# Context rows of the later three batches centred, turned and multiplied with W in two passes of 128 and 103 rows in place of three of 77

## The chip, the cores and the metric

The kernel runs on one core of a Trainium2 chip. The metric is the device time of one execution in microseconds (us). TensorE (PE in the profile) multiplies, and its weight loads are listed apart as PEld. VectorE is DVE, ScalarE is ACT, GpSimd is POOL, and SyncE (SP) only issues DMAs here.

## What is computed

For 4 batches of 2048 tokens with 512 features, each token attends over the 77 context rows of its batch, and a linear layer follows. Both branches are normalised first and both are added back with a gate:

```python
def _L0_xattn_ref(hidden_states, visual_hidden_state):
    fusion_scores = jnp.einsum('bsd,bvd->bsv', hidden_states, visual_hidden_state)
    fusion_probs = jax.nn.softmax(fusion_scores, axis=-1)
    fusion_output = jnp.einsum('bsv,bvd->bsd', fusion_probs, visual_hidden_state)
    return fusion_output
...
x = x + jnp.tanh(g_xattn[0]) * _L0_xattn_ref(_layernorm(x, axis=-1), ctx_1024)
x = x + jnp.tanh(g_ffn[0]) * _L0_ffn_ref(_layernorm(x, axis=-1), L0_ffn_W, L0_ffn_b, L0_ffn_lora_down, L0_ffn_lora_up, L0_ffn_down_aux, L0_ffn_up_aux)
return x
```

`_L0_ffn_ref` multiplies with W plus a low-rank product and adds a bias. All numbers are float32.

## The kernel before

The tokens are cut into T = 64 tiles of 128 rows, TB = 16 tiles to a batch. One loop, `all_tiles`, runs on every engine over t = 0 to 63; `step(t, k)` is the work of a tile, with parts of tiles t - 1, t - 2 and t + 2 laid beside it by hand. The order on each engine is exactly the order of the code, and engines meet through semaphores.

In a step TensorE multiplies the tile's two float parts (a high part and a rest, in `xT`) with `wc`, which holds W side by side with the centred and turned context rows of the batch (24 matmuls, L555). It turns the softmax weights of the tile before (`p_transpose`, L563) and multiplies them with `stacks` (6 matmuls, L581 and L586). `stacks` holds the gated context rows v and their product with W, v*W, each as a high part and a rest, spread by copies over the partitions so that two matmuls take all products; it has two halves, for even and odd batches.

What each batch needs of its context is prepared in the second half of the batch before, by the `prep` functions and a few lines of `step`, at fixed tiles t % 16: rows read and scaled at 8 (STATS) and 9 (ROWS), centred at 10 (CENTRE, DVE L677), turned by four TensorE transposes at 11 (TURN, L522) and taken from PSUM into `ct` by ACT (L394) and DVE (L682), multiplied with W at 12 (PRODUCT, twelve matmuls of 512 columns, L531), and the product taken into `v_hi` and `v_lo` at 13 (TAKE). At 15 (SWITCH) ACT copies `ct` into the columns of `wc` (`ctx_columns`, two copies, L401). This happens three times, each time with 77 rows (V). Batch 0 is prepared before the loop.

The DMAs that matter all go through the one queue of SyncE. It works by units of two tiles. `unit(u)` waits for the output of tiles 2u and 2u + 1, stores it, and loads x (`load_x`) and turned x (`load_xt`) of unit u + 4 into the place that has come free:

```python
for u in range(B * NU - 1):
    n, k = u // NU, u % NU
    if n < B - 1:
        if k == 1:

            sp.wait_ge(v_lo_ok, 2 * n + 2)
            load_ctx(n + 1)
        if k == NU - 2:
            stack(n + 1)
    unit(u)
```

So the next batch's context rows (`c_rows`, 77 rows of 2 KB) are loaded ahead of units 1, 9 and 17, and `v_hi` and `v_lo` are copied into `stacks` by five DMAs (77, 13, 64, 13 and 64 rows of 4 KB, `stack`) ahead of units 6, 14 and 22. ACT converts the turned x of tile t + 2 in step t (`x_hi`, L408) and waits there for that unit's load; it does so ahead of writing the softmax weights of tile t (`probabilities`, L430), for which TensorE's next `p_transpose` waits.

Of the kernel before, what the change touches and what calls it, by code (L numbers as in the profile page):

```python
# [19 lines left out]
def build_kernel(nc, x, xt_in, ctx_in, W, b_gates, low_in, low_out, out):  # L20
# [18 lines left out]
    FIRST = DMAS + 1  # L39
    assert TB == 2 * HB and V + R <= 96 and D == 512  # L40

# [3 lines left out]
    with ExitStack() as stack:  # L45
# [28 lines left out]

        c_rows = sb("c_rows", [V, D])
        c_bn = sb("c_bn", [V, 6])
        c_mv = sb("c_mv", [V, 2])
        c_cent = sb("c_cent", [V, D])
        ct = sb("ct", [P, 2, KC, V], F32R)
        v_hi = sb("v_hi", [V, 2 * D], F32R)  # L80
        v_lo = sb("v_lo", [V, 2 * D], F32R)

# [25 lines left out]
        c_ps = ps("c_ps", [P, D])  # L108
        ct_ps = c_ps[:, 0:KC * V].rearrange("p (c v) -> p c v", c=KC)

# [21 lines left out]
        def cw_ps(n):  # L132

            return a_ps[0:V, :] if n == 0 else c_ps[0:V, :]

# [32 lines left out]
        def all_tiles(step, prep, until=T + 1):  # L168

            for t in range(until):  # L170
                step(t, t)
                if t % TB >= HB and t < T - TB:
                    prep(t // TB + 1, t % TB)

        def switches(t, k):

            return t % TB == k and t < T - TB

        def real(t):
# [15 lines left out]
        def stack_landed(n):  # L195

            return 16 * (DMAS * (n // 2 + 1) + (FIRST - DMAS if n % 2 == 0 else 0))

# [10 lines left out]
        def _(sp):  # L209
# [11 lines left out]
            def stack_hi(n, cols):  # L221

                hi, to = v_hi[:, cols].bitcast(F32), stacks[:, n % 2, :, cols].bitcast(F32)
                for rows, source in ((to[0:V, 0, :], hi), (to[96:K0, 0, :], hi[Q:V, :]), (to[0:Q, 1, :], hi[0:Q, :])):
                    sp.dma_start(rows, source).then_inc(stacked[n % 2], 16)

            def stack_lo(n, cols):

                lo, to = v_lo[:, cols].bitcast(F32), stacks[:, n % 2, :, cols].bitcast(F32)
                for rows, source in ((to[V:V + R, 0, :], lo[Q:V, :]), (to[Q:P, 1, :], lo[0:Q, :])):  # L230
                    sp.dma_start(rows, source).then_inc(stacked[n % 2], 16)

# [5 lines left out]

            def stack(n):

                if n < 2:
                    sp.wait_ge(zeroed, 1)
                else:
                    sp.wait_ge(y_ready, TB * (n - 1))
                sp.wait_ge(v_hi_ok, 2 * n + 1)
                stack_hi(n, slice(0, 2 * D))
                sp.wait_ge(v_lo_ok, 2 * n + 2)
                stack_lo(n, slice(0, 2 * D))

# [19 lines left out]
            sp.wait_ge(v_hi_ok, 1)  # L269
            stack_hi(0, slice(0, D))  # L270
# [4 lines left out]
            stack_lo(0, slice(0, D))  # L275
            first_stack_lo()
# [23 lines left out]
        def _(pool):  # L300
# [9 lines left out]
            def first_columns():  # L310

                pool.wait_ge(ct_lo_ok, 1)
                for part in range(2):
                    pool.tensor_copy(wc[:, :, part, D:D + V], ct[:, part, :, :].bitcast(F32)).then_inc(c_cols, 1)

# [51 lines left out]
        def _(act):  # L367
            act.dma_start(b_row[:, D:D + 2], b_gates[D:D + 2].partition_broadcast(P)).then_inc(ld_gates, 16)
            act.dma_start(c_rows[:, :], ctx_in[0]).then_inc(ld_ctx, 16)
            act.dma_start(low_out_sb[:, :], low_out).then_inc(ld_out, 16)  # L370
# [5 lines left out]
            def ctx_rows_hi(n):  # L376

                act.wait_ge(ld_ctx, 16 * n + 16)
                if n == 0:
                    act.wait_ge(tg_ok, 1)  # L380
                else:
                    act.wait_ge(stacked[(n - 1) % 2], stack_landed(n - 1))
                act.activation(v_hi[:, 0:D], c_rows[:, :], ACT.Copy, scale=tg[0:V, 0:1]).then_inc(v_hi_ok, 1)

            def ctx_product_hi(n):

                act.wait_ge(cw_mm, n + 1)
                act.activation(v_hi[:, D:2 * D], cw_ps(n), ACT.Copy, scale=tg[0:V, 0:1]).then_inc(v_hi_ok, 1)

            def prep(n, k):  # L390
                if k == TURN:

                    act.wait_ge(c_tr, n + 1)
                    act.activation(ct[:, 0, :, :], ct_ps, ACT.Copy).then_inc(ct_hi_ok, 1)  # L394

            def ctx_columns(n):

                act.wait_ge(s_ready, TB * n)
                act.wait_ge(ct_lo_ok, n + 1)
                for part in range(2):  # L400
                    act.activation(wc[:, :, part, D:D + V], ct[:, part, :, :].bitcast(F32), ACT.Copy).then_inc(c_cols, 1)  # L401

# [37 lines left out]
            def step(t, k):  # L440
# [12 lines left out]
                if real(t - 1) and t != T - 1:  # L453
                    variance(t - 1, k - 1)
                if switches(t, STATS):
                    ctx_rows_hi(t // TB + 1)
                if switches(t, TAKE):
                    ctx_product_hi(t // TB + 1)
# [44 lines left out]
        def _(pe):  # L503
# [11 lines left out]
            def prep(n, k):  # L515
                if k == TURN:

                    pe.wait_ge(c_centred, n + 1)
                    if n:
                        pe.wait_ge(v_lo_ok, 2 * n)  # L520
                    for c in range(KC):
                        mm = pe.transpose(ct_ps[:, c, :], c_cent[:, c * P:(c + 1) * P], ident[0:V, 0:V])  # L522
                    mm.then_inc(c_tr, 1)
                if k == PRODUCT:
# [4 lines left out]
                    for c in range(KC):  # L529
                        for lhs, rhs in ((0, 0), (0, 1), (1, 0)):  # L530
                            mm = pe.matmul(cw_ps(n), ct[:, lhs, c, :], wc[:, c, rhs, 0:D],  # L531
                                           start=(m == 0), stop=(m == 3 * KC - 1))
                            m += 1
                    mm.then_inc(cw_mm, 1)

            def first_product():

                pe.wait_ge(ct_lo_ok, 1)
                for c in range(KC + 1):
                    if c < KC:  # L540
                        pe.wait_ge(w_hi_ok, c + 1)
                        for lhs in range(2):
                            pe.matmul(cw_ps(0), ct[:, lhs, c, :], wc[:, c, 0, 0:D], start=(c == 0 and lhs == 0),  # L543
                                      stop=False)
                    if c:
                        pe.wait_ge(w_lo_ok, c)
                        mm = pe.matmul(cw_ps(0), ct[:, 0, c - 1, :], wc[:, c - 1, 1, 0:D], start=False, stop=(c == KC))  # L547
                mm.then_inc(cw_mm, 1)
# [42 lines left out]
            def step(t, k):  # L591
                if real(t):
# [4 lines left out]
                    if k % TB == 0:  # L597
                        pe.wait_ge(c_cols, 2 * (t // TB) + 2)
                    x_product(t, k, 1, range(0, 1))
# [54 lines left out]
        def _(dve):  # L654
            dve.memset(expd[:, :, :], 0.0).then_inc(expd_ok, 1)

            def ctx_rows_lo(n):

                dve.wait_ge(c_own, 2 * n + 1)
                dve.wait_ge(v_hi_ok, 2 * n if n else 1)  # L660
                dve.scalar_tensor_tensor(out=v_lo[:, 0:D], in0=c_rows[:, :], scalar=tg[0:V, 0:1],
                                         in1=v_hi[:, 0:D].bitcast(F32), op0=ALU.mult, op1=ALU.subtract)\
                    .then_inc(v_lo_ok, 1)

            def ctx_mean(n):
                dve.bn_aggr(c_mv[:, :], c_bn[:, :]).then_inc(c_own, 1)

            def prep(n, k):
                if k == STATS:
                    dve.wait_ge(ld_ctx, 16 * n + 16)  # L670
                    dve.bn_stats(c_bn[:, :], c_rows[:, :]).then_inc(c_own, 1)
                if k == ROWS:
                    ctx_rows_lo(n)
                    ctx_mean(n)
                if k == CENTRE:
                    dve.wait_ge(c_own, 2 * n + 2)
                    dve.tensor_scalar(c_cent[:, :], c_rows[:, :], c_mv[:, 0:1], None, ALU.subtract)\  # L677
                        .then_inc(c_centred, 1)
                if k == TURN:

                    dve.wait_ge(ct_hi_ok, n + 1)
                    dve.tensor_tensor(ct[:, 1, :, :], ct_ps, ct[:, 0, :, :].bitcast(F32), ALU.subtract)\  # L682
                        .then_inc(ct_lo_ok, 1)
                if k == TAKE:

                    dve.wait_ge(v_hi_ok, 2 * n + 1)
                    dve.scalar_tensor_tensor(out=v_lo[:, D:2 * D], in0=cw_ps(n), scalar=tg[0:V, 0:1],
                                             in1=v_hi[:, D:2 * D].bitcast(F32), op0=ALU.mult, op1=ALU.subtract)\
                        .then_inc(v_lo_ok, 1)
# [169 lines left out]
```

## Time and profile before

| | |
|---|---|
| median of three runs | 313.3 us (312.91 to 313.48) |
| the profiled execution, its own time | 313.07 us |
| its span (first to last instruction) | 311.3 us |
| TensorE matmul busy | 302.0 us, 97% of the span |
| VectorE, ScalarE, GpSimd busy | 75%, 60%, 73% |
| DMA traffic | 56.39 MB, 181 GB/s on the mean |

Busy shares are means over the span. The granted TensorE clock is given as a share of 2.4 GHz, and its mean is 0.995. A profile's rows name source lines of the kernel before. The profiled execution took 0.2 us less than the median, and 1.8 us of it lie outside the span.

### The profile page before, as it was taken

The page shows a single profiled execution, that of the slowest core. Times are in us where ns is not written, and L with a number is a line of the kernel's source. Part 1 is how long each engine was busy: PE and PEld are TensorE (multiplying, and loading weights), DVE is VectorE, ACT ScalarE, POOL GpSimd, SP SyncE. Part 2 cuts the span into 40 slices and gives each one's busy share as a digit, 9 for nine tenths or more (in the row PEclk, how much of TensorE's full clock was granted, in tenths as well). Part 3 has the DMA queues.
Part 4 walks back from the last instruction along what each step waited for, and adds up shares of the span by engine and source line. Part 5 has one row for each costly group of instructions (what it writes and reads, how often), then busy time and mean ns, then how long its engine had stood idle before and what let it go on. Part 6 is the DMA issues. An engine that isn't in the chain of part 4 may idle for free.

```text
span 311.3 us, 6483 instructions
## 1 busy us (share of the span) xinstructions
PE 302.0 (97%) x2086; PEld 286.1 (92%) x2086; DVE 235.0 (75%) x743; ACT 187.5 (60%) x546; POOL 226.5 (73%) x276
## 2 busy tenths in 40 slices
PE   5999999999999999999999999999999999999992
PEld 3779999998999999999899999999899999999992
DVE  2887778895787887798497778888588777777765
ACT  3665656664576656666466566656466656566552
POOL 3747887788487777877577877778478778877763
PEclk9999999999999999999999999999999999999998
DMA  5845455345594455555294565544197554444013
GB/s 162 305 147 225 151 187 175 149 174 205 182 272 175 166 187 177 204 202 205 73 266 192 202 226 202 204 171 162 76 274 254 203 201 150 169 179 170 27 59 135
DMA packets 16614, 56.39 MB, mean 181 GB/s; under 512 B 2129, under 2 KB 2129, under 8 KB 16580
## 3 DMA queue, kind: packets, MB, share of 16 engines
q1 hardware_dynamic: 15856, 54.64, 50.5%
q10 hardware_dynamic: 724, 1.32, 1.3%
q8 instruction: 17, 0.28, 0.4%
q14 instruction: 17, 0.14, 0.1%
HBM read 35.84 MB, written 16.78 MB: 169 GB/s over the span
## 4 chain that ended last, share of the span: by engine, by line
PE 94%; DMA 2%; DVE 1%; ACT 1%; issue 0%; POOLq 0%; ACTq 0%; POOL 0%; DVEq 0%
PE y_ps L555 66%; PE y_ps L586 10%; PE a_ps L581 10%; PE c_ps L531 3%; PE y_ps L563 2%; DMA c_rows<-in_ctx 2%; PE y_ps L626 1%; PE y_ps L631 1%; PE a_ps L543 1%; PE c_ps L522 1%; PE y_ps L647 0%; PE a_ps L547 0%; PE y_ps L508 0%; DVE o_sb L753 0%; DVE v_lo L818 0%
## 5 line engine op out<-in xcount | busy, mean ns | idle before, releaser
L555 PE MATMUL y_ps<-wc,xT 128*128 128x334 f32 (+1 forms) x1536 | 228.2, 302 | 0.0
L555 PEld LDWEIGHTS y_ps<-wc,xT 128*128 128x128 f32 x1536 | 214.4, 189 | 2.1
L334 POOL TENSOR_TENSOR x_bias<-x,bias_g 128x512 f32<-128x512 f32 x63 | 81.4, 1292 | 63.1 <-DVE x L715 63.1
L322 POOL TENSOR_TENSOR xT<-xt_raw,xT 128x512 fp32r<-128x512 f32 x64 | 83.1, 1298 | 0.1
L423 ACT ACTIVATE expd<-y_ps,neg_max,rs 128x77 f32<-128x77 f32 x64 | 26.6, 416 | 80.2 <-DVE neg_max L705 80.2
L437 ACT ACTIVATE squares<-x,x_nmean 128x512 f32<-128x512 f32 x64 | 46.4, 725 | 16.4 <-DVE x_nmean L723 16.4
L350 POOL TENSOR_TENSOR rs<-stat_eps,half_neg 128x2 f32<-128x2 f32 (+1 forms) x67 | 46.0, 687 | 5.2
L753 DVE SCALAR_TENSOR_TENSOR o_sb<-y_ps,rs,x_bias 128x512 f32<-128x512 f32 x64 | 48.0, 750 | 1.4 <-issue 0.8
L586 PEld LDWEIGHTS y_ps<-stacks,pT 109*128 109x128 f32 (+1 forms) x256 | 39.8, 191 | 5.4
L715 DVE SCALAR_TENSOR_TENSOR x<-a_ps,x_sb 128x512 f32<-128x512 f32 x64 | 43.6, 682 | 0.2 <-PE a_ps L581 0.2
L694 DVE BATCH_NORM_STATS2 bn<-x_sb 128x6 f32<-128x512 f32 x64 | 43.8, 684 | 0.0
L736 DVE TENSOR_TENSOR pT<-y_ps,pT 13x128 fp32r<-13x128 f32 x62 | 18.0, 291 | 32.1 <-ACT pT L414 32.1
L586 PE MATMUL y_ps<-stacks,pT 109*128 109x256 f32 (+1 forms) x256 | 41.0, 282 | 0.0
L581 PE MATMUL a_ps<-stacks,pT 109*128 109x512 f32 (+1 forms) x128 | 40.3, 396 | 0.0
L408 ACT ACTIVATE xT<-xt_raw 128x512 fp32r<-128x512 f32 x63 | 39.2, 622 | 0.0
L702 DVE TENSOR_REDUCE s_max<-y_ps 128x1 f32<-128x77 f32 x64 | 14.9, 233 | 20.7 <-PE y_ps L555 20.3
L430 ACT ACTIVATE p_ext<-expd,e_inv 128x154 f32<-128x154 f32 x64 | 26.5, 414 | 0.7 <-DVE e_inv L730 0.5
L414 ACT ACTIVATE pT<-y_ps 96x128 fp32r<-96x128 f32 x62 | 16.5, 266 | 9.6 <-PE y_ps L563 8.7
L581 PEld LDWEIGHTS a_ps<-stacks,pT 109*128 109x128 f32 (+1 forms) x128 | 19.7, 190 | 0.2 <-issue 0.2
L739 DVE TENSOR_TENSOR pT<-y_ps,pT 64x128 fp32r<-64x128 f32 x62 | 17.5, 283 | 1.9
L415 ACT ACTIVATE pT<-y_ps 64x128 fp32r<-64x128 f32 x62 | 16.6, 268 | 1.5
L563 PE MATMUL y_ps<-ident,p_ext 128*96 128x128 f32 x62 | 16.8, 271 | 0.5 <-ACT p_ext L430 0.5
(80 smaller groups left out, 193.7 us busy)
## 6 DMA issues: line engine op xcount, KB each, us to landing
x_sb<-in_x SPq DMA_DIRECT2D x32, 512.0 KB, 4.2
xt_raw<-in_xt SPq DMA_DIRECT2D x31, 512.0 KB, 5.1
out<-o_sb SPq DMA_DIRECT2D x31, 512.0 KB, 3.0
stacks<-v_hi SPq DMA_DIRECT2D x3, 308.0 KB
stacks<-v_hi SPq DMA_DIRECT2D x3, 256.0 KB
stacks<-v_lo SPq DMA_DIRECT2D x3, 256.0 KB
w_rows<-in_w SPq DMA_DIRECT2D x2, 256.0 KB, 6.1
w_rows<-in_w ACTq DMA_DIRECT2D x2, 256.0 KB, 6.8
```

What stands on the lines that cost most here:

```text
L322: pool.tensor_tensor(xT[:, k % TRING, 1, :, :], xt_raw[:, k % XRING // UNIT, k % UNIT, :, :], xT[:, k % TRING, 0, :, :].bitcast(F32), ALU. ...
L334: pool.tensor_tensor(x1_bias[:, q, :], x1[:, j, :], bias_g[:, :], ALU.add).then_inc(x1b_ready, 1)
L350: pool.tensor_tensor(rs[:, q, a:b], stat_eps[:, q, a:b], half_neg[:, a:b], ALU.pow).then_inc(rs_ready, 1)
L408: act.activation(xT[:, k % TRING, 0, :, :], xt_raw[:, k % XRING // UNIT, k % UNIT, :, :], ACT.Copy)\
L423: act.activation(expd[:, j, 0:V], scores(k), ACT.Exp, bias=neg_max[:, j:j + 1], scale=rs[:, k % 4, 0:1], accum_out=e_sum[:, j:j + 1]).then ...
L437: act.activation(squares[:, k % 2, :], x1[:, k % 2, :], ACT.Square, bias=x1_nmean[:, k % 2:k % 2 + 1], scale=D ** -0.5, accum_out=stat[:, ...
L555: mm = pe.matmul(y_half(k, h)[:, 0:n], xT[:, k % TRING, part, c, :], wc[:, c, w, h * H:h * H + n], start=(c == 0 and part == 0 and w == 0) ...
L581: mm = pe.matmul(a_ps[:, :], pT[0:rows[s], k % 2, s, :], stacks[0:rows[s], pair, s, 0:D], start=(s == 0), stop=(s == 1))
L586: mm = pe.matmul(y_half(k, h)[:, 0:H], pT[0:rows[s], k % 2, s, :], stacks[0:rows[s], pair, s, D + h * H:D + (h + 1) * H], start=False, sto ...
L694: dve.bn_stats(bn[:, k % 2, :], x_sb[:, k % XRING, :]).then_inc(bn_ok, 1)
L715: dve.scalar_tensor_tensor(out=x1[:, j, :], in0=a_ps[:, :], scalar=1.0, in1=x_sb[:, k % XRING, :], op0=ALU.mult, op1=ALU.add, accum_out=x1 ...
L753: dve.scalar_tensor_tensor(out=o_sb[:, q, :].rearrange("p (h d) -> p h d", h=2), in0=y_both(k), scalar=rs[:, (k + 3) % 4, 1:2], in1=x1_bia ...
```

## The change

The context rows of batches 1, 2 and 3 (231 rows) are handled in two passes: 128 rows (batch 1, and 51 rows of batch 2, here TAIL) in the second half of batch 0, and 103 rows (26 of batch 2, 77 of batch 3) in the second half of batch 1. In the second half of batch 2 nothing is prepared but the columns of `wc`. `ct` is kept twice, `c_rows`, `v_hi`, `v_lo` are 128 rows high, and the copies into `stacks` are cut and moved to match.

```diff
+    PACK = (V, P, (B - 1) * V - P)
+    TAIL = P - V
...
-        ct_ps = c_ps[:, 0:KC * V].rearrange("p (c v) -> p c v", c=KC)
+        ct_all = c_ps[:, :].rearrange("p (c v) -> p c v", c=KC)
...
-                if t % TB >= HB and t < T - TB:
+                if t % TB >= HB and t < T - 2 * TB:
                     prep(t // TB + 1, t % TB)
...
             def load_ctx(n):
-                sp.dma_start(c_rows[:, :], ctx_in[n:n + 1].rearrange("o v d -> (o v) d")).then_inc(ld_ctx, 16)
...
+                at = V + (n - 1) * P
+                sp.dma_start(c_rows[0:PACK[n], :], ctx_in.rearrange("b v d -> (b v) d")[at:at + PACK[n], :])\
+                    .then_inc(ld_ctx, 16)
...
+            def stack_head(n):
+
+                both = slice(0, 2 * D)
+                copy(n, slice(0, TAIL), 0, v_hi, V, both)
+                copy(n, slice(0, TAIL), 1, v_hi, V, both)
+                copy(n, slice(Q, Q + TAIL), 1, v_lo, V, both)
...
+            def stack_rest(n):
+
+                both = slice(0, 2 * D)
+                copy(n, slice(TAIL, V), 0, v_hi, 0, both)
+                copy(n, slice(96, K0), 0, v_hi, Q - TAIL, both)
+                copy(n, slice(TAIL, Q), 1, v_hi, 0, both)
+                copy(n, slice(V, V + R), 0, v_lo, Q - TAIL, both)
+                copy(n, slice(Q + TAIL, P), 1, v_lo, 0, both)
...
-                if n < B - 1:
-                    if k == 1:
-
-                        sp.wait_ge(v_lo_ok, 2 * n + 2)
-                        load_ctx(n + 1)
-                    if k == NU - 2:
-                        stack(n + 1)
+                if n < 2 and k == 1:
+                    sp.wait_ge(v_lo_ok, 2 * n + 2)
+                    load_ctx(n + 1)
+                if n == 0 and k == NU - 2:
+                    rows_cast(1)
+                    stack_hi(1, 0, slice(0, 2 * D))
+                    stack_lo(1, 0, slice(0, 2 * D))
+                if n == 1 and k == 1:
+                    sp.wait_ge(y_ready, TB)
+                    stack_head(2)
+                if n == 1 and k == NU - 2:
+                    rows_cast(2)
+                    stack_rest(2)
+                if n == 2 and k == 1:
+                    sp.wait_ge(y_ready, 2 * TB)
+                    stack_hi(3, V - TAIL, slice(0, 2 * D))
+                    stack_lo(3, V - TAIL, slice(0, 2 * D))
                 unit(u)
...
+                if n == 2:
+                    act.wait_ge(stacked[0], 16 * (FIRST + 3))
...
+                    if n == 2:
+                        act.activation(wc[:, :, part, D:D + TAIL], ct[:, 1, part, :, V:P].bitcast(F32), ACT.Copy)\
+                            .then_inc(c_cols, 1)
+                        act.activation(wc[:, :, part, D + TAIL:D + V], ct[:, 0, part, :, 0:V - TAIL].bitcast(F32), ACT.Copy)\
+                            .then_inc(c_cols, 1)
```

Three places show how the order moves. First the DMA queue of SyncE at the start of batch 1, before the change; the rows are from the store of unit 8 to the loads of unit 14 (output, x, turned x, and the context rows):

```order
L254 DMA out<-o_sb 128x1024 [waits out_ready]
L211 DMA x_sb<-in_x 128x1024
L215 DMA xt_raw<-in_xt 128x1024 [waits xl_ready]
L219 DMA c_rows<-in_ctx 77x512 [waits v_lo_ok]
L254 DMA out<-o_sb 128x1024 [waits out_ready]
L211 DMA x_sb<-in_x 128x1024
L215 DMA xt_raw<-in_xt 128x1024 [waits xl_ready]
```

The same place of the same queue after the change:

```order
L288 DMA out<-o_sb 128x1024 [waits out_ready]
L229 DMA x_sb<-in_x 128x1024
L233 DMA xt_raw<-in_xt 128x1024 [waits xl_ready]
L238 DMA c_rows<-in_ctx 103x512 [waits v_lo_ok]
L243 DMA stacks<-v_hi 51x1024 [waits y_ready]
L243 DMA stacks<-v_hi 51x1024
L243 DMA stacks<-v_lo 51x1024
L288 DMA out<-o_sb 128x1024 [waits out_ready]
L229 DMA x_sb<-in_x 128x1024
L233 DMA xt_raw<-in_xt 128x1024 [waits xl_ready]
```

The context load has 103 rows in place of 77, and three copies of 51 rows now stand between it and the store of unit 9 and the loads of unit 13.

TensorE in the second half of batch 2, before the change; from the second step shown, four transposes of the centred context stand ahead of a tile, and twelve matmuls of the product a step later:

```order
L581 MATMUL a_ps<-stacks,pT 128x512 x2
L586 MATMUL y_ps<-stacks,pT 128x256 x4
L555 MATMUL y_ps<-wc,xT 128x256 x6
L522 MATMUL c_ps<-ident,c_cent 128x77 x4
L555 MATMUL y_ps<-wc,xT 128x334 x3
L563 MATMUL y_ps<-ident,p_ext 96x128
L555 MATMUL y_ps<-wc,xT 128x334 x9
L555 MATMUL y_ps<-wc,xT 128x256 x6
L581 MATMUL a_ps<-stacks,pT 128x512 x2
L586 MATMUL y_ps<-stacks,pT 128x256 x4
L555 MATMUL y_ps<-wc,xT 128x256 x6
L531 MATMUL c_ps<-wc,ct 77x512 x12
```

The same place after the change:

```order
L635 MATMUL a_ps<-stacks,pT 128x512 x2
L640 MATMUL y_ps<-stacks,pT 128x256 x4
L609 MATMUL y_ps<-wc,xT 128x256 x6
L609 MATMUL y_ps<-wc,xT 128x334 x3
L617 MATMUL y_ps<-ident,p_ext 96x128
L609 MATMUL y_ps<-wc,xT 128x334 x9
```

The four transposes and the twelve matmuls are gone from this batch and nothing takes their place. In the two passes that stay, the transposes are 128x128 and 128x103 and the product 128x512 and 103x512, at the same places as before.

## Rows read from the trace of the kernel before

**Rows 1.** Waits of TensorE in the loop: us in total, times, longest

```profile
PE y_ps L563 <- ACT p_ext L430: 0.5, 1, 0.5
```

**Rows 2.** The chain that ended last: start us, us, what (third pass)

```profile
206.72 2.10 PE y_ps L555 x15
...
211.05 2.09 PE y_ps L555 x15
...
215.69 2.09 PE y_ps L555 x15
...
222.81 2.09 PE y_ps L555 x15
```

**Rows 3.** Timeline of TensorE, five places: start us, us, line, tile, shape

```profile
7.72 0.78 PE L522 MATMUL c_ps<-ident,c_cent 77*128 77x77 f32 x4 [0.50 <-DVE c_cent L677]
...
68.33 0.63 PE L581 MATMUL a_ps<-stacks,pT 109*128 109x512 f32 x2
...
69.99 0.43 PE L522 MATMUL c_ps<-ident,c_cent 77*128 77x77 f32 x4
...
146.95 2.96 PE L531 MATMUL c_ps<-wc,ct 128*77 128x512 f32 x12
...
305.08 0.64 PE L586 MATMUL y_ps<-stacks,pT 109*128 109x256 f32 x4
```

**Rows 4.** Groups by shape: xcount, busy us, mean ns of one, idle before

```profile
L581 PE MATMUL a_ps<-stacks,pT 109*128 109x512 f32 x64 | 25.3, 395 | 0.0
...
L581 PEld LDWEIGHTS a_ps<-stacks,pT 128*128 128x128 f32 x64 | 12.2, 190 | 0.0
...
L531 PEld LDWEIGHTS c_ps<-wc,ct 128*77 128x77 f32 x36 | 5.1, 145 | 2.6
...
L812 DVE SCALAR_TENSOR_TENSOR wc<-y_ps,tg,wc 128x512 fp32r<-128x512 f32 x4 | 2.8, 747 | 1.0 <-ACT wc L497 0.9
...
L821 DVE SCALAR_TENSOR_TENSOR stacks<-a_ps,tg,stacks 64x512 fp32r<-64x512 f32 x1 | 0.7, 744 | 0.0
```

**Rows 5.** Timeline of ACT and of weight loads in step 31

```profile
160.56 0.81 ACT L401 ACTIVATE wc<-ct 128x308 fp32r<-128x308 f32 x2 [0.44 <-PE y_ps L555]
...
162.19 0.41 ACT L430 ACTIVATE p_ext<-expd,e_inv 128x154 f32<-128x154 f32 x1
...
163.04 0.13 PEld L563 LDWEIGHTS y_ps<-ident,p_ext 128*96 128x96 f32 x1
```

**Rows 6.** DMA packets from 115.3 to 123.9, 106.7 to 115.3, 80.8 to 97 us

```profile
DMA packets 432, 1.57 MB, mean 183 GB/s; under 512 B 48, under 2 KB 48, under 8 KB 432
...
DMA packets 522, 1.76 MB, mean 204 GB/s; under 512 B 59, under 2 KB 59, under 8 KB 520
...
DMA packets 1165, 4.11 MB, mean 254 GB/s; under 512 B 165, under 2 KB 165, under 8 KB 1164
```

**Rows 7.** Windows: busy by engine; the last three are PEclk, DMA share, GB/s

```profile
84.00:85.00 1.00, 1.00 (x9) 0.92 (x8) 0.96 (x4) 0.05 (x1) 1.00 (x1) 1.00 1.00 401
...
87.00:88.00 1.00, 1.00 (x8) 1.00 (x7) 0.71 (x4) 0.77 (x4) 0.92 (x3) 1.00 1.03 160
...
112.00:113.00 1.00, 1.00 (x9) 0.97 (x8) 0.70 (x2) 0.97 (x3) 1.00 (x1) 1.00 0.46 160
...
308.00:309.00 1.00, 0.00 (x0) 0.00 (x0) 0.75 (x1) 0.00 (x0) 0.00 (x0) 0.69 0.68 258
```

**Rows 8.** Timeline around units 9 and 13: SyncE's queue, ACT, weight loads

```profile
108.46 0.41 SPq L219 DMA_DIRECT2D c_rows<-in_ctx  x1
...
116.30 0.79 SPq L215 DMA_DIRECT2D xt_raw<-in_xt  x1
...
128.09 0.62 ACT L408 ACTIVATE xT<-xt_raw 128x512 fp32r<-128x512 f32 x1
128.61 0.42 ACT L430 ACTIVATE p_ext<-expd,e_inv 128x154 f32<-128x154 f32 x1
...
129.65 0.12 PEld L563 LDWEIGHTS y_ps<-ident,p_ext 128*96 128x96 f32 x1
```

More of the change, by code:

```diff
@@ L39, in build_kernel @@
     FIRST = DMAS + 1
-    assert TB == 2 * HB and V + R <= 96 and D == 512
+    PACK = (V, P, (B - 1) * V - P)
+    TAIL = P - V
+    assert TB == 2 * HB and V + R <= 96 and D == 512 and B == 4 and 0 < TAIL < Q and V <= PACK[2] <= P
     x_units = x.rearrange("b (u p n) d -> (b u) p n d", p=P, n=UNIT)
@@ L73, in build_kernel @@
         wc = sb("wc", [P, KC, 2, D + VP], F32R)
[L75 to L81, printed above, removed]
+        c_rows = sb("c_rows", [P, D])
+        c_bn = sb("c_bn", [P, 6])
+        c_mv = sb("c_mv", [P, 2])
+        c_cent = sb("c_cent", [P, D])
+        ct = sb("ct", [P, 2, 2, KC, P], F32R)
+        v_hi = sb("v_hi", [P, 2 * D], F32R)
+        v_lo = sb("v_lo", [P, 2 * D], F32R)
         stacks = sb("stacks", [P, 2, 2, 2 * D], F32R)
@@ L132, in cw_ps @@
         def cw_ps(n):
-            return a_ps[0:V, :] if n == 0 else c_ps[0:V, :]
+            return a_ps[0:V, :] if n == 0 else c_ps[0:PACK[n], :]
         def up_bank():
@@ L177, in switches, with packs, columns_done @@
             return t % TB == k and t < T - TB
+        def packs(t, k):
+            return t % TB == k and t < T - 2 * TB
+        def columns_done(n):
+            return 2 * n + 2 + (2 if n >= 2 else 0)
         def real(t):
@@ L195, in stack_landed @@
         def stack_landed(n):
-            return 16 * (DMAS * (n // 2 + 1) + (FIRST - DMAS if n % 2 == 0 else 0))
+            return 16 * (FIRST, DMAS, FIRST + 3 + DMAS, 2 * DMAS)[n]
         def unit_turn(t, k, ring):
@@ L218, in load_ctx, with copy, stack_hi, stack_lo @@
             def load_ctx(n):
-                sp.dma_start(c_rows[:, :], ctx_in[n:n + 1].rearrange("o v d -> (o v) d")).then_inc(ld_ctx, 16)
[L221 to L231, printed above, removed]
+                at = V + (n - 1) * P
+                sp.dma_start(c_rows[0:PACK[n], :], ctx_in.rearrange("b v d -> (b v) d")[at:at + PACK[n], :])\
+                    .then_inc(ld_ctx, 16)
+            def copy(n, rows, s, source, at, cols):
+                sp.dma_start(stacks[rows, n % 2, s, cols].bitcast(F32),
+                             source[at:at + rows.stop - rows.start, cols].bitcast(F32)).then_inc(stacked[n % 2], 16)
+            def stack_hi(n, at, cols):
+                copy(n, slice(0, V), 0, v_hi, at, cols)
+                copy(n, slice(96, K0), 0, v_hi, at + Q, cols)
+                copy(n, slice(0, Q), 1, v_hi, at, cols)
+            def stack_lo(n, at, cols):
+                copy(n, slice(V, V + R), 0, v_lo, at + Q, cols)
+                copy(n, slice(Q, P), 1, v_lo, at, cols)
+            def stack_head(n):
[10 more added lines that the diff above has]
+                copy(n, slice(Q + TAIL, P), 1, v_lo, 0, both)
             def first_stack_lo():
@@ L530, in prep @@
                         for lhs, rhs in ((0, 0), (0, 1), (1, 0)):
[L531 removed]
+                            mm = pe.matmul(cw_ps(n), ct_part(n, lhs)[:, c, :], wc[:, c, rhs, 0:D],
                                            start=(m == 0), stop=(m == 3 * KC - 1))
@@ L542, in first_product @@
                         for lhs in range(2):
-                            pe.matmul(cw_ps(0), ct[:, lhs, c, :], wc[:, c, 0, 0:D], start=(c == 0 and lhs == 0),
+                            pe.matmul(cw_ps(0), ct_part(0, lhs)[:, c, :], wc[:, c, 0, 0:D], start=(c == 0 and lhs == 0),
                                       stop=False)
@@ L546, in first_product @@
                         pe.wait_ge(w_lo_ok, c)
-                        mm = pe.matmul(cw_ps(0), ct[:, 0, c - 1, :], wc[:, c - 1, 1, 0:D], start=False, stop=(c == KC))
+                        mm = pe.matmul(cw_ps(0), ct_part(0, 0)[:, c - 1, :], wc[:, c - 1, 1, 0:D], start=False, stop=(c == KC))
                 mm.then_inc(cw_mm, 1)
```

59 lines of the change are left out of this document (31 added, 28 removed).

## Prediction

> **What bounds the kernel now.** I read the waits of TensorE first. In the whole loop it waits once, for 0.5 us in the first step [rows 1]; after that it never stands still until the last tiles. The chain of work that ended last then says what a step costs. An ordinary step lasts 4.33 us (206.72 to 211.05), the step with the four transposes 4.64 us (211.05 to 215.69), and the step with the twelve product matmuls 7.12 us (215.69 to 222.81) [rows 2]. So a pass over the context costs TensorE 0.31 + 2.79 = 3.10 us, every bit of it on the path, and there are three. What the other engines and the queues do is free as long as they stay inside a cover that I work out below for each.
>
> **What the change removes.** One pass, 3.10 us.
>
> **What grows on TensorE.** The two passes left have more rows. The product's moving side stays 512 columns; only the weights widen from 77 to 128 and 103 columns. A weight load of 128 columns takes 190 ns against 145 ns for 77 [rows 4]. It lies under the matmul before it: the twelve matmuls start (2.96 - 0.395) / 11 = 0.233 us apart, and two matmuls of the same 512 columns with 128-column weights start 0.63 - 0.395 = 0.235 us apart [rows 3, 4]. The product gets no dearer. The Trainium skill ("TensorE: Matmul & The Clock Gate", section LDWEIGHTS) has weight loading grow with columns, at columns / 1.2 ns; uncovered that would be 24 loads of up to 43 ns more, an estimate of 1.0 us, and the saving that much smaller. The loads' durations agree with the direction, the spacing of the matmuls shows them covered.
> The transposes move more columns, 128 and 103 against 77. In proportion to columns, the 0.31 us grows by 0.20 and by 0.10 us. The low end is nothing (the weight loads, 128 columns wide either way, set their pace); for the high end I take the same four transposes at the start of the program, 0.78 against 0.43 us [rows 3], so 0.35 us for each pass. I take 0.3 us, with 0 to 0.7 as ends. TensorE alone thus gives 3.10 - 0.3 = 2.8 us back.
>
> **What grows elsewhere at no cost.** DVE and ACT work on more partitions in the same time: 744 ns for 64 rows, 747 ns for 128 [rows 4]. The copies of `ct` go from 308 to 512 elements, some 0.2 us on ACT and on DVE, in the step before the long product, which covers both. In step 31 ACT makes four column copies (204 and 104 elements, twice) in place of two of 308. The two take 0.81 us [rows 5]. The four move the same elements and add two fixed parts, between 0.2 us (if they overlap like the present pair) and 0.6 us (if not). The softmax weights are ready at 162.60 and TensorE loads them at 163.04 [rows 5], which leaves 0.44 us, of which a hand-over needs 0.06. I take 0.2 us, hidden; at the high end 0.2 us would show. The copies of batch 3 into `stacks` move from unit 22 to unit 17, with rows of the same counts as today, and nothing waits for them there.
>
> **Where I expect a new wait.** A transfer does not always use all 16 DMA engines. In a stretch with only one store and two loads, each of 128 rows, 48 packets are under 512 B, that is 3 x 16: each engine that works on a transfer writes one small packet when it is done [rows 6]. With a load of 77 context rows beside the three there are 59, so 11 engines for 77 rows. With two such sets of three and the five copies of 77, 13, 64, 13 and 64 rows there are 165 = 96 + 11 + 13 + 16 + 13 + 16 [rows 6]. The number of engines is the largest one up to 16 that divides the rows. The new shapes are bad for that: 103 is prime, so one engine carries the whole context load of pass two, and 51 = 3 x 17, so three engines carry each of the three copies ahead of unit 9. (26 and 13 rows still get 13, and 128 rows get 16, better than now.)
> An engine moves 401 / 16 = 25.1 GB/s at a share of 1.00 [rows 7]. The context load is 103 x 2 KB on one engine, 8.4 us. The three copies are 3 x 17 rows of 4 KB on each of theirs, 209 KB, 8.3 us. The queue is worked off in order on each engine, so the store of unit 9 and the loads of unit 13 follow: three times 32 KB, 3.9 us. Today the engines are through with unit 12 at about 112.4 us (share 0.46 in 112 to 113 [rows 7]), and the context load is issued at 108.46 [rows 8], so it waits there already. If the single engine is one of the three, the turned x of unit 13 lands at 112.4 + 8.4 + 8.3 + 3.9 = 133.0 us. ACT converts its first tile at 128.09 [rows 8]. It stands 4.9 us, in front of the softmax weights of tile 24. TensorE has 129.65 - 129.03 = 0.62 us to spare there, 0.56 without the hand-over, and so stands still for 4.35 us. Behind ACT's conversion nothing is queued that gets a wait of its own: ACT's other wait for the copies themselves stands later in the step, and they are down by 129.1. DVE's output of tile 22 needs the store of unit 9, down at 130.4, inside the same wait. Unit 14 follows 3.9 us after unit 13, at 136.9, and its first tile is converted two steps and the wait after 128.09, at 141.1, so the wait comes once. Its length depends on differences alone, and the times that the first pass shifts by 0.2 us don't change it.
> Whether the engines are the same ones no row tells. I take it that they are, and price the other case as a rival. The Trainium skill ("DMA: Bandwidth & Descriptors", section "Why a DMA increments its semaphore by 16 and not by 1") gives the divisor rule too, and the rows agree with it (59 and 165); it adds that SyncE's transfers take the lowest-numbered engines, which no row here shows. By it the wait is the 4.35 us above; without it there is none.
>
> **The clock behind the wait.** TensorE's last matmul ends at 305.72 [rows 3], and between 308 and 309 the granted clock is already 0.69 on the mean, on its way from 2.4 to 1.2 GHz [rows 7]. So standing still for 4.35 us can bring it down. Work at the lower level takes about twice as long (0.78 against 0.43 us for the four transposes, if the first is at that level). The price lies between nothing and a whole step's work done at the lower level, 4.33 us more. I take a third of that, 1.4 us, since the fall may come late in the wait and a stalled TensorE has all its inputs ready behind it.
>
> **Sum.** 313.07 - 3.10 + 0.3 + 4.35 + 1.4 = 316.0 us against the profiled execution, which is 0.2 us under the median of 313.3. I leave it at 316.0.
>
> **Rivals.**
> *The load hides the narrow transfers* (the other side). The three copies and the context load sit on different engines, or a lone engine is faster than one among 16. The mechanism's place is ACT at 128.1: unit 13 would be there by 112.4 + 3.9 = 116.3 on an engine with nothing else, so up to 11.8 us of added work on one engine costs nothing, and 12.4 us nothing on TensorE. One of the two jobs (8.4 or 8.3 us) stays under, both (16.7) don't. The change then gives its 2.8 us: 310.3 us. For it: no row names an engine. 12 in 100.
> *The wait without the clock.* 313.07 - 2.8 + 4.35 = 314.6 us. 20 in 100.
> *The copies inside SBUF are slower.* While the five copies run today, the engines are as busy but move 160 GB/s in place of 401 [rows 7], 10 GB/s each. If three engines go at that rate, 209 KB take 20.9 us in place of 8.3, and the wait grows by 12.6 us: about 328 us. Against it: in that stretch 64 rows go to and from the same half of the partitions with 16 engines at once; three engines should not get in each other's way. 8 in 100, and half-way cases (a few us) are in my forecast's upper side.
> *Forecast*, wait with some loss of clock, 315 to 320 us: 57 in 100. The 3 left are a wait so short that it and the saving cancel.
>
> **How the numbers follow.** The forecast's own spread comes from the clock (0 to 4.3 us), the transposes (0 to 0.7) and slightly slower copies (2 us). The range 312.5 to 320.0 takes in the wait with and without the clock and a shortened wait; it leaves out the hidden case (12) and the slow copies (8). A measurement of this kernel can tell about 0.2% (0.6 us) from no change. Faster: the hidden case, 0.12. Same: 0.03. Slower: 0.85.
>
> **What would show it.** In the changed kernel's trace the step of pass one should be about 0.2 us longer at the transposes and unchanged at the product, and batch 2 should have no long step. A window on the context load of pass two should show it landing 8 us after its start, with a DMA share near 1/16. ACT should wait at the conversion of tile 26 for the turned x, and TensorE for `p_ext` once, around 130 us, for 4 to 5 us, with the granted clock under 1.00 just after. If TensorE's waits there are missing, the engines were not shared and the time is near 310; if the wait is over 10 us, the copies are the slow ones.

## The result, and the profile after

The changed kernel takes 317.91 us (median of four runs, 317.42 to 318.01) against 313.39 us for the kernel before in the same comparison (four runs, 312.91 to 313.67). The ratio is 1.0143, with a 95% interval of 1.0122 to 1.0165. It is slower, inside the predicted range and 1.9 us above the predicted 316.0. Its profiled execution took 317.83 us.

The page of the changed kernel, from the span to the slices, and the shares of the chain that ended last:

```profile
span 315.8 us, 6441 instructions
...
PE 300.2 (95%) x2070; PEld 285.7 (90%) x2070; DVE 233.1 (74%) x737; ACT 187.4 (59%) x545; POOL 226.6 (72%) x276
...
PE   5999999999999999389999999999999999999992
...
PEclk9999999999999999969999999999999999999998
...
PE 87%; DMA 7%; DVE 2%; ACT 1%; issue 1%; POOL 0%; POOLq 0%; ACTq 0%; DVEq 0%
```

There is one hole in TensorE's row, in slices 17 and 18 (7.9 us each), and a dip of the granted clock just behind it. The waits of the changed kernel (us in total, times, longest) name what was late; they answer to [rows 1]:

```profile
ACT xT L462 <- DMA xt_raw<-in_xt: 7.6, 1, 7.6
...
DVE o_sb L809 <- DMA out<-o_sb: 5.7, 1, 5.7
...
PE y_ps L609 <- DVE o_sb L809: 4.8, 1, 4.8
...
PE y_ps L617 <- ACT p_ext L484: 1.8, 2, 1.3
```

Two transfers were late: a store (DVE can't overwrite `o_sb`) and a load of turned x (ACT can't convert it). TensorE stood for DVE first and then, three matmuls later, for ACT's softmax weights. The timeline of the changed kernel around the wait, first TensorE, then its weight loads at `p_transpose`, then DVE and ACT (start us, us, and in brackets the idle time before and what ended it):

```profile
127.71 0.87 PE L609 MATMUL y_ps<-wc,xT 128*128 128x256 f32 x6
133.35 1.17 PE L609 MATMUL y_ps<-wc,xT 128*128 128x334 f32 x3 [4.77 <-DVE o_sb L809]
135.85 0.45 PE L617 MATMUL y_ps<-ident,p_ext 128*96 128x128 f32 x1 [1.33 <-ACT p_ext L484]
...
124.42 0.12 PEld L617 LDWEIGHTS y_ps<-ident,p_ext 128*96 128x96 f32 x1
135.85 0.15 PEld L617 LDWEIGHTS y_ps<-ident,p_ext 128*96 128x96 f32 x1 [1.75 <-ACT p_ext L484]
141.68 0.12 PEld L617 LDWEIGHTS y_ps<-ident,p_ext 128*96 128x96 f32 x1
146.00 0.13 PEld L617 LDWEIGHTS y_ps<-ident,p_ext 128*96 128x96 f32 x1
...
132.45 0.75 DVE L809 SCALAR_TENSOR_TENSOR o_sb<-y_ps,rs,x_bias 128x512 f32<-128x512 f32 x1 [5.70 <-DMA out<-o_sb]
...
134.85 0.63 ACT L462 ACTIVATE xT<-xt_raw 128x512 fp32r<-128x512 f32 x1 [7.56 <-DMA xt_raw<-in_xt]
```

The four weight loads measure the whole damage: from 124.42 to 146.00 there are three steps, and they take 21.58 us. In the kernel before the same three take 12.99. I call this "the three steps around the wait" and compare it through the experiments, because it is free of everything else that differs from run to run. Of the 8.59 us, 7.1 lie in the first step (135.85 - 124.42 = 11.43 for 4.31) and 1.5 in the second (141.68 - 135.85 = 5.83), where no wait is listed but the clock is low. The windows of the changed kernel (the last three columns are the granted clock, the DMA share and GB/s) show both:

```profile
112.00:114.00 2.00, 2.00 (x16) 2.00 (x15) 1.21 (x5) 0.62 (x3) 1.92 (x4) 1.00 0.19 60
...
118.00:120.00 2.00, 2.00 (x17) 1.92 (x16) 1.97 (x7) 1.61 (x5) 1.19 (x2) 1.00 1.01 279
...
130.00:132.00 2.00, 0.00 (x0) 0.00 (x0) 0.00 (x0) 0.00 (x0) 0.00 (x0) 1.00 0.06 25
132.00:134.00 2.00, 0.65 (x2) 0.68 (x3) 1.51 (x6) 0.00 (x0) 0.05 (x1) 0.67 0.06 27
134.00:136.00 2.00, 0.67 (x4) 0.25 (x3) 0.84 (x3) 1.15 (x3) 1.22 (x1) 0.50 0.10 35
136.00:138.00 2.00, 2.00 (x8) 2.00 (x8) 0.66 (x3) 1.54 (x5) 1.35 (x3) 0.50 0.07 27
138.00:140.00 2.00, 2.00 (x11) 1.95 (x11) 1.64 (x5) 0.64 (x3) 0.79 (x1) 0.63 0.00 0
```

A share of 0.06 is 1/16: from 130 to 138 us it is mostly a single DMA engine that works, at 25 GB/s, and until 134.85 the core waits for it. At 112 to 114 the share is 0.19, that is 3/16 (and 0.19 again at 114 to 115, with 76 GB/s), although the 103-row load and a 51-row copy are both open: three engines in all, so the load's one is among the copies' three. The chain of the changed kernel follows that one queue back (start us, us, what):

```profile
116.90 17.93 DMA xt_raw<-in_xt
...
134.85 0.05 ACT xT L462
...
135.39 0.42 ACT p_ext L484
...
135.85 0.45 PE y_ps L617
136.29 3.58 PE y_ps L609 x15
```

Turned x of unit 13 is issued at 116.90 and down 17.93 us later; a usual load of it takes about 5. (The queue rows ahead of the prediction end with the loads of unit 13, not 14 as is said there.)

The semaphore events of the same trace have one entry for each engine that finishes its part of a transfer, and they show the shared engine directly. Fifteen engines had stored unit 9 by 123.77 us and brought turned x of unit 13 by 126.89; the sixteenth came at 132.33 and 134.83. The load of 103 rows, on one engine, was down at 121.77, and the last of the copies at 131.07. So one engine did all of it in order: the load (9.3 us, from 112.47, when it was through with unit 12), its part of the copies (9.3 us), and its part of the store and the two loads (3.8 us). The other two engines of the copies were through with them by 122.74, more than 8 us earlier.

The saving is in the trace as well. The chain of the changed kernel at pass one and in batch 2, beside [rows 2]:

```profile
61.25 2.10 PE y_ps L609 x15
...
65.57 2.10 PE y_ps L609 x15
...
70.31 2.10 PE y_ps L609 x15
...
77.39 2.10 PE y_ps L609 x15
...
214.27 2.10 PE y_ps L609 x15
...
218.58 2.11 PE y_ps L609 x15
...
222.90 2.10 PE y_ps L609 x15
```

The steps of pass one start 4.32, 4.74 and 7.08 us apart (before: 4.33, 4.64, 7.12), and batch 2 has ordinary steps only.

### The profile page after: what moved, and what is told of

Read it like the earlier page. It is cut to its first block, busy times and chain, and to the rows that moved or that the text cites. A ratio compares the mean times of both kernels' runs of the same rounds, so it can differ in the third digit from the quotient of the medians.

```text
span 315.8 us, 6441 instructions
## 1 busy us (share of the span) xinstructions
PE 300.2 (95%) x2070; PEld 285.7 (90%) x2070; DVE 233.1 (74%) x737; ACT 187.4 (59%) x545; POOL 226.6 (72%) x276
## 4 chain that ended last, share of the span: by engine, by line
PE 87%; DMA 7%; DVE 2%; ACT 1%; issue 1%; POOL 0%; POOLq 0%; ACTq 0%; DVEq 0%
PE y_ps L609 62%; PE a_ps L635 9%; PE y_ps L640 9%; DMA xt_raw<-in_xt 6%; PE y_ps L617 2%; PE c_ps L585 2%; DMA c_rows<-in_ctx 2%; PE y_ps L680 1%; PE y_ps L685 1%; PE a_ps L597 1%; PE c_ps L576 0%; DVE o_sb L809 0%; DVE x L771 0%; POOL x_bias L378 0%; PE a_ps L601 0%
## 5 line engine op out<-in xcount | busy, mean ns | idle before, releaser
L758 DVE TENSOR_REDUCE s_max<-y_ps 128x1 f32<-128x77 f32 x64 | 15.0, 235 | 23.9 <-PE y_ps L609 23.7
L392 POOL TENSOR_TENSOR stat_eps<-stat,eps 128x2 f32<-128x2 f32 (+1 forms) x67 | 13.3, 199 | 6.4 <-DVE stat L752 3.3
```

## The experiments

For each kernel stand its median, that of the kernel before in the same comparison, the ratio with its 95% interval, and the three steps around the wait. No kernel leaves out a part of the computation; those that start from the kernel before add transfers or tensors that nothing uses, and one adds matmuls whose result nothing reads.

**The context load in two pieces.** Pass two's load in 96 and 7 rows in place of 103 (16 engines and 7, by the divisor rule); the copies stay at three engines. The two waits for the load count one piece more.

```
-                sp.dma_start(c_rows[0:PACK[n], :], ctx_in.rearrange("b v d -> (b v) d")[at:at + PACK[n], :])\
-                    .then_inc(ld_ctx, 16)
+                for a, m in ((0, PACK[n]),) if n < 2 else ((0, 96), (96, PACK[n] - 96)):
+                    sp.dma_start(c_rows[a:a + m, :], ctx_in.rearrange("b v d -> (b v) d")[at + a:at + a + m, :])\
+                        .then_inc(ld_ctx, 16)
```

> The changed kernel, with the context load of 103 rows cut into 96 and 7 rows (16 and 7 engines in place of one). Theory 1 (the load and the three copies of 51 rows add up in the queue of one engine, 9.9 and 9.3 us, and only the sum passes the cover of about 12 us): no wait is left, the kernel gives back the whole 8.6 us of steps 24 to 26, 317.9 - 8.6 = 309.3 us. Rival A (the lone engine of the context load is enough by itself): also about 309.3. Rival B (the three copies on three engines, or SyncE standing in their issue, are enough): the wait stays, 317 to 318 us.

Measured: 309.84 us against 313.09, ratio 0.9895 [0.9874, 0.9916]; the three steps take 13.30 us, and TensorE has no wait for DVE. The load alone, in another number of pieces, turns a loss of 1.4% into a gain of 1.0%. Only 0.36 us of delay is left beside the uncut copies (ACT stands 0.60 us for turned x).

**The copies in two pieces each.** The other half alone: each copy of 51 rows as 48 and 3. The two waits for the copies count three pieces more.

```
-                copy(n, slice(0, TAIL), 0, v_hi, V, both)
-                copy(n, slice(0, TAIL), 1, v_hi, V, both)
-                copy(n, slice(Q, Q + TAIL), 1, v_lo, V, both)
+                for a, b in ((0, 48), (48, TAIL)):
+                    copy(n, slice(a, b), 0, v_hi, V + a, both)
+                    copy(n, slice(a, b), 1, v_hi, V + a, both)
+                    copy(n, slice(Q + a, Q + b), 1, v_lo, V + a, both)
```

> The changed kernel, with each of the three copies of 51 rows cut into 48 and 3 rows (16 and 3 engines), the context load left at 103 rows on one engine. Theory 1 (the two add up on one engine): no wait, 309.3 us. Rival A (the context load is enough): the wait stays, 317 to 318 us. Rival B (the copies or their issue are enough): 309.3 us.

Measured: 310.82 us against 313.09, ratio 0.993 [0.9906, 0.9954]; the three steps take 14.29 us. The waits of TensorE and the timeline of ACT in this kernel:

```profile
PE y_ps L618 <- ACT p_ext L485: 1.3, 2, 0.8
...
129.44 0.63 ACT L463 ACTIVATE xT<-xt_raw 128x512 fp32r<-128x512 f32 x1 [1.59 <-DMA xt_raw<-in_xt]
```

With the 103-row load left on one engine ACT still stands 1.59 us for turned x and TensorE 0.8 us, where the prediction had either job over 3 us inside the cover of 11.8. By the semaphore events the load's engine was through with unit 12 at 113.95, later than the prediction's 112.4, took 9.8 us for the load in place of 8.4, and had another 2.0 us of copies, for the pieces run on it too. The times won back by one cut or the other (8.6 - 0.36 and 8.6 - 1.35) add up to far more than the 8.6 that there are: the jobs queue behind each other, and either one alone almost fits.

**Both in pieces.** The two diffs above together.

> The changed kernel with both cuts: load 96 + 7, copies 48 + 3. All theories: no wait at steps 24 to 26, 309.3 us, which is 4 us (1.3%) faster than the kernel before. If the wait stays here, the number of engines is not the cause at all. The steps should last 4.31 us as in the changed kernel if that small gain came from the change.

Measured: 309.62 us against 313.09, ratio 0.9887 [0.9864, 0.9909]; the three steps take 12.94 us, three ordinary steps of 4.31. This is the change as it was meant, and the fastest median of the study. Its page:

```profile
PE 298.5 (97%) x2070; PEld 284.3 (92%) x2070; DVE 232.8 (76%) x737; ACT 187.3 (61%) x545; POOL 226.4 (73%) x276
```

**The narrow load two units earlier.** Still one transfer of 103 rows, issued ahead of unit 7 in place of unit 9.

```
-                if n < 2 and k == 1:
-                    sp.wait_ge(v_lo_ok, 2 * n + 2)
-                    load_ctx(n + 1)
+                if u in (1, NU - 1):
+                    sp.wait_ge(v_lo_ok, 2 if u == 1 else 4)
+                    load_ctx(1 if u == 1 else 2)
```

> The changed kernel with the context load of 103 rows, uncut, issued one batch edge earlier: ahead of unit 7 in place of unit 9. Nothing else changes. Theory 1: each job alone is under the cover, two units apart they no longer meet, no wait, 309.3 us. If the width alone matters (either job too long by itself): a wait stays, at step 20 to 22 (load) or 24 (copies), and the time is over 312 us.

Measured: 310.1 us against 313.09, ratio 0.9897 [0.9874, 0.992]; the three steps take 12.94 us. The same bytes on the same single engine cost nothing when they don't meet the copies. It is the sum in one queue that costs, not the shape of a transfer as such.

**The transfers alone.** The kernel before, with one 103-row load and three 51-row transfers into spare tensors ahead of unit 9, and all else unchanged. It still has three passes of 77 rows, with their own load ahead of the added transfers, and none of the other parts of the change.

```
+                        if n == 1:
+                            sp.dma_start(spare_c[0:103, :], ctx_in.rearrange("b v d -> (b v) d")[205:308, :]).then_inc(spared, 16)
+                            for i in range(3):
+                                sp.dma_start(spare_v[0:51, i, :], w_rows[V:P, 0:2, :].rearrange("p c d -> p (c d)")).then_inc(spared, 16)
```

> The kernel before, all three passes of 77 rows kept, with four transfers added ahead of unit 9 that nothing uses: a load of 103 context rows and three copies of 51 rows of 4 KB inside the chip's memory (from the rows of W), all into spare tensors. Theory 1 (these transfers alone make the wait): 313.4 + 8.6 = 322.0 us, a little less or more as the copies' source differs. Rival C (the wait needs the change's other parts, such as ACT's added wait for the copies): about 313.4 us.

Measured: 322.27 us against 313.17, ratio 1.0296 [1.0277, 1.0316], so 9.1 us more; the three steps take 21.74 us. TensorE's wait in this kernel:

```profile
PE y_ps L563 <- DVE o_sb L761: 4.6, 1, 4.6
```

The transfers by themselves make the whole loss, with the same two-part wait as in the changed kernel. How long SyncE stands in issuing them is not what sets it in the changed kernel: there turned x of unit 13 was issued in full by 118.91 us, 16 us before its last part came down.

**Two loads of 103 rows.** The kernel before with two such loads, independent of each other, into spare rows. If every transfer picked an engine anew, they would run side by side.

```
+                        if n == 1:
+                            for i in range(2):
+                                sp.dma_start(spare_c[0:103, i, :], ctx_in.rearrange("b v d -> (b v) d")[205:308, :]).then_inc(spared, 16)
```

> The kernel before, with two loads of 103 context rows added ahead of unit 9 into a spare tensor, nothing else. Each runs on one engine for about 9 us (103 is prime). Theory 1 with a fixed choice of engine: both sit on the same engine, 18 to 20 us, and TensorE waits as in the changed kernel, about 313.2 + 7 to 9 = 320 to 322 us. If one-engine transfers take another engine each time: 9 us each stays under the cover (12 us) and the time is 313.2, at most 314.5 us.

Measured: 322.09 us against 313.07, ratio 1.0288 [1.0256, 1.032]; the three steps take 22.25 us. The waits of TensorE and two windows of this kernel:

```profile
PE y_ps L561 <- DVE o_sb L759: 4.9, 1, 4.9
...
116.00:118.00 2.00, 2.00 (x18) 1.98 (x17) 1.57 (x6) 1.72 (x6) 1.29 (x2) 1.00 0.06 25
...
120.00:122.00 2.00, 2.00 (x17) 1.93 (x17) 1.89 (x7) 1.76 (x6) 1.16 (x2) 1.00 0.06 25
```

From 116 to 122 us one engine of sixteen is busy though two loads are open, both issued by 114.1. By the semaphore events they came down one after the other, at 123.18 and 132.79, 9.6 us apart. In this kernel the two one-engine transfers took the same engine.

**The clock kept up.** The changed kernel, with 27 matmuls in TensorE's two waits whose result nothing reads, so that the clock has no reason to fall. They write into PSUM (`c_ps`) that is free then.

```
+            def fill(count):
+                pe.wait_ge(v_lo_ok, 4)
+                for _ in range(count):
+                    pe.matmul(c_ps[:, :], wc[:, 0, 0, 0:P], wc[:, 0, 0, 0:D], start=True, stop=True)
...
+                    if t == 25:
+                        fill(21)
...
+                if t == 25:
+                    fill(6)
```

> The changed kernel, with 27 matmuls that nothing uses put on TensorE where it stands still: 21 ahead of tile 25's first matmuls (4.9 us), 6 ahead of the transpose of tile 24 (1.4 us). They fill the waits and add work of at most a few tenths. Theory 1 with the clock (2.4 us of the 8.6 are work done at the lower clock after standing still): the granted clock stays 1.00 there and the time is 317.9 - 2.4 + up to 0.5, about 315.5 to 316.0 us. Rival D (the clock costs nothing, all 8.6 us are waits): 317.9 us or a little more.

Measured: 316.74 us against 313.17, ratio 1.0125 [1.0107, 1.0142]; the three steps take 20.37 us. The timeline of TensorE and one window of this kernel:

```profile
128.89 4.95 PE L594 MATMUL c_ps<-wc 128*128 128x512 f32 x21
...
136.44 0.31 PE L623 MATMUL y_ps<-ident,p_ext 128*96 128x128 f32 x1 [0.47 <-ACT p_ext L484]
...
134.00:136.00 2.00, 1.97 (x9) 1.35 (x9) 1.40 (x5) 0.56 (x2) 1.30 (x1) 1.00 0.07 27
```

The clock stays at 1.00 where it was 0.50, and the kernel gets back 317.91 - 316.74 = 1.2 us by the medians, 21.58 - 20.37 = 1.2 us in the three steps. That is net: the second step falls from 5.83 to 4.48, the first is 0.11 longer (11.54). The wait stays: 20.37 - 12.94 = 7.4 us. So of the changed kernel's loss about 7.4 us are wait and 1.2 us clock. The cost I expected here was twice that.

**Where the shorter step comes from.** The changed kernel's ordinary steps take 4.314 us in place of 4.327, all along the loop and in every kernel made from it. The tensors after `ct` lie 5.7 KB further on in each partition there. Three kernels made from the one before add an unused tensor of that size at one place and do nothing else: behind `ct`, ahead of `xT`, and behind `xT`. The line is the same in all three:

```
+        spare = sb("spare", [P, 2, KC, 2 * P - V], F32R)
```

Behind `ct`:

> The kernel before with a spare tensor beside ct, so that all later tensors lie at the addresses they have in the changed kernel; no work changes. If the shorter step of the changed kernel (4.314 against 4.326 us, 0.7 us over the kernel) and its earlier first step (0.7 us) come from addresses: 312.0 to 312.8 us and steps of 4.31 us. If they come from the run or from the change's code: 313.4 us and steps of 4.33 us.

Ahead of `xT`:

> The kernel before with the spare tensor of e7 placed just ahead of xT in memory, so only xT and what follows it move; no work changes. If the shorter step (4.314 against 4.326 us) comes from where xT, the softmax weights or what follows them lie: steps of 4.31 us. If it comes from v_hi, v_lo, stacks or x ahead of xT: steps stay 4.33 us. Time 312.4 or 313.2 us.

Behind `xT`:

> The same with the spare tensor placed just behind xT, so that xT stays and what follows it (statistics, softmax weights and their transposes, outputs) moves. If xT's own place is what counts: steps of 4.33 us, 313.2 us. If the place of the softmax weights and their transposes counts: 4.31 us, 312.4 us.

Measured (mean step from the weight loads of `p_transpose` in ten steps of batch 2, the step with the product in pass one, and the times):

| unused tensor | step, us | product step | median | before | ratio |
|---|---|---|---|---|---|
| none (before) | 4.326 | 7.12 | | | |
| behind `ct` | 4.313 | 7.08 | 312.37 (12 runs) | 313.17 | 0.9976 [0.9962, 0.9991] |
| ahead of `xT` | 4.333 | 7.09 | 314.01 (8 runs) | 313.07 | 1.0024 [1.0007, 1.0042] |
| behind `xT` | 4.326 | 7.12 | 313.07 (8 runs) | 313.07 | 1.0006 [0.9992, 1.0021] |
| none (changed) | 4.313 | 7.08 | 317.91 | 313.39 | 1.0143 |

An unused tensor shortens the step by 0.3% or lengthens it by 0.2% (0.3% in batch 1, where the step is 4.340). Moving everything from `v_hi` on shortens it, moving `xT` and what follows lengthens it, moving only what follows `xT` does nothing. So it has to do with where `xT` lies, and also with where something between `ct` and `xT` lies; which tensor that is stays open, and no kernel was run that moves one alone. Nor does every shift count: the two kernels with added transfers have their unused tensors ahead of `c_mv`, 14.3 and 4.1 KB of them, which moves `ct`, `v_hi`, `xT` and all that follows, and their step stays at 4.326. With the tensor ahead of `xT`, the steps from the first to the last `p_transpose` add up to 0.5 us more than before (273.61 for 273.12), and the medians differ by 0.9; the rest is not traced. The time before the first step differs too (22.1 to 23.7 us over the profiled executions), but in no order that follows the addresses.

With this the pass can be priced at equal addresses: 309.62 for both splits against 312.37 for the kernel before with the addresses of the changed one, 2.75 us. The two medians come from different comparisons, whose kernel before differs by 0.1 us.

## Why the prediction was right, and where it was off

The direction and the mechanism were right, and the range held the time. Step by step:

- **The pass on TensorE**, predicted 3.10 - 0.3 = 2.8 us: measured 2.75. That they agree so closely is in part luck: by the steps the pass is worth 3.09 - 0.18 = 2.9 us at equal addresses, and 0.3 us are lost again at the end, which was not in the sum. The transposes grew by 0.12 us in pass one (4.75 for 4.63) and by 0.06 in pass two (4.69), 0.18 together where I took 0.3; the low end, at which their weight loads set the pace and nothing grows, is wrong. The product step stayed at 7.08, that of the kernel before at the same addresses, so the wider weight loads are covered, as the spacing of [rows 3] had it.
- **Step 31's four column copies**, predicted hidden for 0.2 us more: they run from 168.25 to 169.25, 1.00 us for 0.81, and TensorE's weight load still comes 0.23 us behind the softmax weights (before 0.44 [rows 5]). Right.
- **The engines are shared.** Which engines a narrow transfer gets was the open question, and the rival in which the load hides the copies stood on it. The two loads settle it for one-engine transfers; the semaphore events and the two splits taken one by one settle it for this kernel. The Trainium skill ("DMA: Bandwidth & Descriptors", section "Why a DMA increments its semaphore by 16 and not by 1") has SyncE's transfers on the lowest-numbered engines. The runs agree in that the engine is the same one each time (a DMA share of 0.06 with two such loads open); no run here shows its number.
- **The size of the wait** is the step that failed: "turned x of unit 13 lands at 112.4 + 8.4 + 8.3 + 3.9 = 133.0 us", and so "TensorE ... stands still for 4.35 us". It measured 7.4. The wait and its place were right, its terms too small. The step of tile 24 starts 0.9 us earlier in the changed kernel's profile (124.42 for 125.32), so 133.0 stands for 132.1 there, and the load came down at 134.83, 2.7 us late. The semaphore events give each term. I had the engine free of unit 12 at 112.4, 111.5 in the changed kernel's time, from a mean over sixteen engines; the shared one is the last of them, and was free at 112.47, 1.0 us later. (It is the last in the kernel before as well: 113.97, where the others are through by 112.70.) The context load took 9.3 us for 8.4 and the copies 9.3 for 8.3, both 22.5 to 22.7 GB/s on the mean in place of 25.1. The unit's three transfers took 3.8 for 3.9. Why the narrow transfers stay under 25.1 GB/s, which the windows from 130 us on do show, is open. (7.4 us is by the kernel with the clock held up; the first step's own excess is 7.1.)
- **What is held first** was the store of unit 9, not turned x: the prediction had it "down at 130.4, inside the same wait". It released DVE at 132.45, and TensorE went on with three matmuls at 133.35 before it stood again for turned x. I take it that it cost nothing of its own, since `p_transpose` at 135.85 waited for ACT, and ACT for turned x; no run has one without the other.
- **The clock**, predicted 1.4 us with "a third" of a step's work at the lower level: measured 1.2 us with the clock held up, 1.5 us by the second step of the changed kernel's own rows. A third of a step was a guess between two ends, so that it came close is luck. The row under the doubling, 0.78 against 0.43 us, doesn't show it: the granted clock of the kernel before is 1.00 from 7 to 8 us. The changed kernel does: fifteen matmuls take 3.58 us where they took 2.10, most of them at 0.50. TensorE stood from 128.6 us; the clock was 1.00 in 130 to 132, 0.67 on the mean in 132 to 134, and 0.50, which is 1.2 GHz, up to 138.
- **Slow copies inside SBUF**, the 328 us rival: wrong. On the shared engine the copies took 9.3 us, no longer than the context load of the same size.
- **Not in the sum at all**: the shorter step, about 0.7 us over the loop, and 0.3 us lost at the end. There the last step but one takes 4.4 us for 4.1 in every kernel without the third pass, with TensorE's weight loads idle for 0.26 us that the changed kernel's trace puts down to issue. The cause of that idle time stays open. The 0.3 us is contained in the 2.75 above. The shorter step hid a part of the wait's miss: without it the time would have been about 318.7, still inside the range.

The sum with the measured terms is 313.4 - 2.75 + 7.4 + 1.2 - 0.75 = 318.5, against 317.9; the 0.6 us between them is about what the start of the loop varies from profile to profile (0.7 us earlier here than before), and is not traced further.

## What to carry to other kernels

Look at the number of rows of every DMA, for one transfer that runs on one engine or three is not slow where it is issued but in the transfers queued behind it, here a store and two loads of other data, 20 us later. Split a prime number of rows (103 as 96 and 7), or issue it where the queue of that engine is empty; either gave the 1.0 to 1.1% that the change was made for. And add up narrow transfers by engine over the whole stretch that has to recover: the copies alone cost 0.36 us here, the load alone 1.35, and both together 8.6.

## What the hardware showed that I had not expected

**A DMA issue can be held back.** SyncE's queue in the changed kernel, ahead of units 9 and 13 (start us, us of the issue):

```profile
107.62 0.32 SPq L238 DMA_DIRECT2D c_rows<-in_ctx  x1
107.99 5.64 SPq L243 DMA_DIRECT2D stacks<-v_hi  x2
113.67 1.24 SPq L243 DMA_DIRECT2D stacks<-v_lo  x1
114.96 1.21 SPq L288 DMA_DIRECT2D out<-o_sb  x1
116.22 0.64 SPq L229 DMA_DIRECT2D x_sb<-in_x  x1
116.90 2.01 SPq L233 DMA_DIRECT2D xt_raw<-in_xt  x1
```

Two copies of 51 rows take 5.64 us to issue, behind the 103-row load. With both in pieces, the first two copies take 1.23 us:

```profile
108.67 0.91 SPq L239 DMA_DIRECT2D c_rows<-in_ctx  x2
109.62 1.23 SPq L244 DMA_DIRECT2D stacks<-v_hi  x2
```

In the kernel with two loads of 103 rows, the store of unit 9 behind them takes 6.60 us to issue:

```profile
116.00 6.60 SPq L256 DMA_DIRECT2D out<-o_sb  x1
```

It ends at 122.60, 0.6 us before the first of the two loads is down, and in the windows above fifteen engines have nothing to do meanwhile. So a full engine seems to stop SyncE itself, and with it the transfers that would have used the fifteen others. That the issue took longer is shown, why it did is not, and no run shows a cost of it: what everything waited for was the sixteenth engine.

**Addresses move the step.** An unused tensor of 5.7 KB per partition changed a step of TensorE by -0.013 or +0.007 us in batch 2 (4.313 and 4.333 for 4.326), and the kernel by -0.8 or +0.9 us by the medians. That is more than the bound of 0.6 us under which I called a time the same, so a change that resizes a tensor can't be read to a fraction of a per cent without a kernel that has the addresses and nothing else.
